# Cross value sums on eight blocks in one place, and the causal mask added inside a fused maximum

## What is computed

```python
att = jnp.einsum('bhqd,bhkd->bhqk', q, k) * scale
att = jnp.where(causal[None, None], att, -jnp.inf)
y = jnp.einsum('bhqk,bhkd->bhqd', jax.nn.softmax(att, axis=-1), v)
attc = jnp.einsum('bhqd,bhkd->bhqk', qc, kc) * scale
y = y + jnp.einsum('bhqk,bhkd->bhqd', jax.nn.softmax(attc, axis=-1), vc)
...
x = x + jnp.tanh(g_xattn[0]) * _L0_xattn_ref(_layernorm(x, axis=-1), ctx_512, ...)
```

## Time and profile before

| | us |
|---|---|
| median of 3 runs | 1542.45 (1542.35 to 1543.42) |
| the profiled execution | 1540.59 |
| its span, first to last instruction | 1538.5 |
| TensorE busy | 1426.7 (93%) |
| VectorE busy | 1145.7 (74%) |
| GpSimd busy | 901.9 (59%) |
| ScalarE busy | 896.0 (58%) |

### The profile page before, as it was taken

The page is one execution under the profiler, slowest core; times in us unless marked ns, Lnnn a source line. Parts: engine busy times, 40 slices in busy tenths (PEclk is TensorE's granted clock), DMA queues, the critical chain, the costliest instruction groups (busy, mean ns, idle before and its releaser), DMA issues.

```text
span 1538.5 us, 36199 instructions
## 1 busy us (share of the span) xinstructions
PE 1426.7 (93%) x11288; PEld 948.6 (62%) x11288; DVE 1145.7 (74%) x3026; ACT 896.0 (58%) x1907; POOL 901.9 (59%) x1643
## 2 busy tenths in 40 slices
PE   4899999999999999999999999999979989898997
PEld 3556556655566566555655665665546778787675
DVE  6777887878778887878788787878644555565686
ACT  3466676666667676666667666665723555565210
POOL 4245566664756666575756657475654555665782
PEclk8899999999999999999999999999999999999999
DMA  6745454545454554645464454545555565454794
GB/s 169 198 131 138 140 151 141 172 135 165 135 160 146 157 169 120 183 133 151 134 177 144 136 180 126 159 134 172 178 152 160 169 221 170 150 153 143 230 351 165
DMA packets 184123, 250.01 MB, mean 162 GB/s; under 512 B 32024, under 2 KB 134560, under 8 KB 183936
## 3 DMA queue, kind: packets, MB, share of 16 engines
q1 hardware_dynamic: 149680, 185.60, 42.0%
...
## 4 chain that ended last, share of the span: by engine, by line
PE 63%; DVE 18%; ACT 11%; issue 5%; DMA 2%; POOL 1%; SPq 0%; DVEq 0%; ACTq 0%; POOLq 0%
PE vector_bank L2025 8%; PE pv_self L1529 8%; DVE nmax L1288 7%; PE scalar_bank L1465 7%; PE vector_bank L1502 5%; PE vector_bank L1575 4%; PE vector_bank L1439 3%; PE vector_bank L1499 3%; ACT q L857 3%; PE scalar_bank L1452 2%; PE scalar_bank L1455 2%; PE scalar_bank L1453 2%; ACT parts L866 2%; PE scalar_bank L2012 2%; ACT parts L873 2%
## 5 line engine op out<-in xcount | busy, mean ns | idle before, releaser
L1288 DVE TENSOR_REDUCE nmax<-vector_bank 128x1 f32<-128x384 f32 (+4 forms) x832 | 511.2, 639 | 74.4 <-PE vector_bank L1502 70.0
L929 ACT ACTIVATE pt<-scalar_bank 128x512 f32<-128x512 f32 x640 | 362.7, 605 | 175.6 <-PE scalar_bank L1465 167.1
L746 POOL TENSOR_SCALAR_AFFINE_SELECT pt<-pt 128x256 f32<-128x256 f32 (+1 forms) x640 | 222.7, 362 | 206.4 <-ACT pt L929 184.4
L1465 PE MATMUL scalar_bank<-stack 99*64 99x512 bf16 (+4 forms) x1280 | 284.2, 319 | 2.3 <-ACT pt L929 1.0
L1502 PE MATMUL vector_bank<-stack 96*128 96x128 bf16 (+3 forms) x1024 | 244.0, 301 | 0.0
L1854 POOL DMA_INDIRECT rows<-pt x143 | 139.1, 973 | 117.3 <-DVE pt L1983 63.2
L1499 PE MATMUL vector_bank<-tri,ident_b 128*128 128x128 bf16 (+2 forms) x704 | 175.3, 249 | 21.5 <-DMA stack<-qk_scratch 10.5
L1529 PE MATMUL pv_self<-pt,vst 128*32 128x512 f32 (+3 forms) x2048 | 161.1, 438 | 0.1
L705 POOL DMA_INDIRECT rows<-xn,slot x128 | 132.8, 1037 | 44.2 <-issue 26.3
L1499 PEld LDWEIGHTS vector_bank<-tri,ident_b 128*128 128x128 bf16 x704 | 67.0, 97 | 145.2 <-DVE nmax L1288 59.9
L2025 PE MATMUL vector_bank<-pt 128*128 128x128 f32 x1144 | 151.2, 275 | 0.1
...
## 6 DMA issues: line engine op xcount, KB each, us to landing
...
```

What stands on the lines that cost most here:

```text
L746: pool.affine_select(out=v, in_=v, compare_op=ALU.is_ge, fill=0.0, base=0, pattern=pat, channel_multiplier=-1).then_inc(masked, 1)
L929: act.activation(dst, bank(kind, b, ("st", c, k))[:, :], ACT.Exp, scale=SCALE).then_inc(scalar_drained, 1)
L1288: dve.tensor_reduce(dst, src, axis=AX, op=ALU.max, negate=True).then_inc(vector_drained, 1)
L1465: return pe.matmul(out, stack[c][0:rows, head, key0:key0 + nk], stack[c][0:rows, head, q0:q0 + nq], start=True, stop=True, **kw)
```

## The change

Cross value sums. A half's cross products now stand in one place, at k = 14: eight products of 64 rows (one head's keys) by 32 output rows, the even heads on rows 0 to 63 into `pv_cross`, the odd ones on rows 64 to 127 into `pv_self`. `vcst` shrinks to 32 columns a pair, and the zeros go. ScalarE copies both banks at k = 15 (before: one at k = 18, at (1, 3) and at the end of c = 1). Since the bank `pv_self` is shared, the self products of (c, 0) move from k = 16 and 20 to 18 and 22. The turned cross sums move from the ends of the halves, the start of the next batch and (1, 6) to (0, 19), (0, 23), (1, 18) and (1, 21). `normalise` writes every second head of `yc`, which is one tile now.

Mask. For the 16 units a half with one head, TensorE's product with `tri` is left out, and VectorE's reduction is replaced by `tensor_tensor_reduce`: it adds `hidden_keys` (bf16, zeros and the triangle at its end) to the bank, multiplies by -1, writes the result back into the bank, and takes the minimum into `nmax`. GpSimd fills `hidden_keys` once.

```diff
@@ -85,7 +85,8 @@
 LN_SUMS = {(0, 21): 0, (0, 22): 1, (0, 23): 2, (1, 0): 3}
 LN_AGGREGATE = (1, 2)
 
-CUR_UNITS = {(1, 6): ("tU", 0, 1, "x"), (1, 11): ("tU", 0, 1, "s"),
+CUR_UNITS = {(1, 11): ("tU", 0, 1, "s"), (0, 19): ("tU", 0, 0, "x"), (0, 23): ("tU", 0, 1, "x"),
+             (1, 18): ("tU", 1, 0, "x"), (1, 21): ("tU", 1, 1, "x"),
              (0, 2): ("mT", 0, 1), (0, 16): ("mT", 1, 0), (1, 2): ("mT", 1, 1)}
 NEXT_UNITS = {(1, 8): ("v", 0), (1, 9): ("v", 1), (1, 10): ("vc",), (1, 13): ("xT", 0), (1, 15): ("xT", 1), (1, 16): ("mT", 0, 0)}
 LN_ROWS = {(1, 7): 0, (1, 9): 1, (1, 11): 2, (1, 12): 3}
...
@@ -181,19 +183,19 @@
         prev, cur, nxt = PARTS[kind]
         out = [("xT0", 0), ("xT0", 1)] if kind == "pro" else []
         if prev:
-            out += [("tU", 1, 1, "x"), ("tU", 1, 1, "s")]
+            out += [("tU", 1, 1, "s")]
         if cur:
             out += [("sm", 1, k) for k in range(SM_PRE)]
         for k in range(NST):
             out += besides(kind, 0, k)
         if cur:
-            out += [("tU", 0, 0, "x"), ("tU", 0, 0, "s")]
+            out += [("tU", 0, 0, "s")]
         if nxt:
             out += [("sm", 0, k) for k in range(SM_PRE)]
         for k in range(NST):
             out += besides(kind, 1, k)
         if cur:
-            out += [("tU", 1, 0, "x"), ("tU", 1, 0, "s")]
+            out += [("tU", 1, 0, "s")]
         return out
 
     def of_current(names):
...
@@ -212,10 +214,13 @@
     BY_SCALAR = [("yT", k) for k in range(KC)] + [("rT", t) for t in range(QT)]
     VD = Events(lambda kind: [n for n in vector_units(kind) if n not in BY_SCALAR], LB)
     TAKEN = Events(lambda kind: BY_SCALAR if PARTS[kind][0] else [], LB)
-    PV = Events(of_current([(w, c, g) for c in range(KC) for g in range(2) for w in ("x", "s")]), LB, credit=8)
+    PV = Events(of_current([(w, c, g) for c in range(KC) for w in ("x", "s") for g in range(2)]), LB, credit=8)
     MASKED = Events(of_current([(c, g, s) for c in range(KC) for g in range(2) for s in range(10)]), LB)
     YADD = Events(lambda kind: ([(1, 1)] if PARTS[kind][0] else []) + ([(0, 0), (0, 1), (1, 0)] if PARTS[kind][1] else []),
                   LB, credit=4)
+    NORM = Events(lambda kind: ([("s", 1, 1)] if PARTS[kind][0] else []) +
+                  ([("x", 0, 0), ("x", 0, 1), ("s", 0, 0), ("s", 0, 1), ("x", 1, 0), ("x", 1, 1), ("s", 1, 0)]
+                   if PARTS[kind][1] else []), LB)
     SPLIT = Events(of_next([0, 1]), LB)
     MSPLIT = Events(lambda kind: ([(0, 1), (1, 0), (1, 1)] if PARTS[kind][1] else []) +
                     ([(0, 0)] if PARTS[kind][2] else []), LB)
...
@@ -273,7 +278,8 @@
         VROW = HU * (D + 1) + 32 - D - 1
         vst_all = sb("vst", [P, QT * KC * HU * 32])
         vst = vst_all[:, 0:3 * QT * VROW].rearrange("p (s t w) -> p s t w", s=3, w=VROW)
-        vcst = sb("vcst", [P, 3, HU // 2, 64])
+        vcst_all = sb("vcst", [P, 3 * HU // 2 * 64])
+        vcst = vcst_all[:, 0:3 * HU // 2 * 32].rearrange("p (s a d) -> p s a d", s=3, d=32)
         nmax = [sb(f"nmax{c}", [P, QT, HU, 2]) for c in range(KC)]
         mres = sb("mres", [P, HEAD_GROUP, 2, QT])
         mparts = [sb(f"mparts{g}", [P, HEAD_GROUP, MROWS, 2, QT], BF16) for g in range(2)]
...
@@ -283,9 +289,9 @@
         ct = [ct_all[:, g, :, :] for g in range(2)]
         usum_all = sb("usum", [P, 4, T])
         usum = {(w, g): usum_all[:, 2 * g + i, :] for i, w in enumerate(("x", "s")) for g in range(2)}
-        recip = {w: sb(f"recip_{w}", [P, QT, HEAD_GROUP]) for w in ("x", "s")}
+        recip = {(w, g): sb(f"recip_{w}{g}", [P, QT, HEAD_GROUP]) for w in ("x", "s") for g in range(2)}
         y = sb("y", [P, QT, H, D])
-        yc = [sb(f"yc{g}", [P, QT, HEAD_GROUP, D]) for g in range(2)]
+        yc = sb("yc", [P, QT, HU, D])
         yT = sb("yT", [P, KC, T])
         xr = sb("xr", [P, QT, C])
         xn2 = [sb(f"xn2{i}", [P, QT, ROW]) for i in range(2)]
...
@@ -878,10 +885,12 @@
                     act.wait_ge(vector_filled, VU.upto(kind, b, ("tU", 0, g, w)))
                 elif g == 0:
                     act.wait_ge(vector_filled, VU.start(kind, b))
-                elif PARTS[kind][0]:
+                elif w == "s" and PARTS[kind][0]:
                     act.wait_ge(vector_filled, VU.upto(kind, b, ("tU", 1, 1, w)))
+                else:
+                    act.wait_ge(vector_filled, VU.start(kind, b))
                 act.wait_ge(pv_filled, PV.upto(kind, b, (w, c, g)))
-                act.activation(usum[w, g][:, :], (pv_cross if w == "x" else pv_self)[:, :], ACT.Copy).then_inc(pv_drained, 1)
+                act.activation(usum[w, g][:, :], (pv_cross if (w, g) == ("x", 0) else pv_self)[:, :], ACT.Copy).then_inc(pv_drained, 1)
 
             def turned_rows(kind, b, name):
 
...
@@ -955,16 +964,14 @@
                             finished_rows(kind, b, c, k)
                         if (c, k) == ROUTE_EXP and prev:
                             route_exp(b)
-                        if c == 1 and k == 3:
-                            unnormalised(kind, b, "x", 0, 1)
                         if c == 1 and k == 8:
                             unnormalised(kind, b, "s", 0, 1)
-                        if k == 18:
-                            unnormalised(kind, b, "x", c, 0)
+                        if k == 15:
+                            for i in range(2):
+                                unnormalised(kind, b, "x", c, i)
                     if cur:
                         unnormalised(kind, b, "s", c, 0)
                         if c == 1:
-                            unnormalised(kind, b, "x", 1, 1)
                             unnormalised(kind, b, "s", 1, 1)
                     elif nxt:
                         for i in (2, 3):
...
@@ -1090,10 +1097,10 @@
             def cross_values(kind, b):
                 ps = filled(kind, b, ("vc",))
                 twin = 1 + (LN.upto(kind, b, 0) - 1) % 2
-                for half_, col in ((0, 0), (1, 32)):
+                for half_ in range(2):
                     rows = slice(half_ * TC, (half_ + 1) * TC)
                     last = dve.tensor_tensor(
-                        vcst[rows, 0:twin + 1:twin, :, col:col + D],
+                        vcst[rows, 0:twin + 1:twin, :, 0:D],
                         ps[rows, 0:C].rearrange("p (s a i d) -> p s a i d", s=KC, i=2, d=D)[:, :, :, half_, :],
                         bcv[rows, :].rearrange("p (s a i d) -> p s a i d", s=KC, i=2, d=D)[:, :, :, half_, :], ALU.add)
                 last.then_inc(vector_drained, 1)
...
@@ -1285,6 +1292,12 @@
                         w = (qt + 1) * P
                         src = ps[:, 0:n * w].rearrange("p (h t) -> p h t", t=w)
                         dst = nmax[c][:, qt, h:h + n, 0]
+                    if what == "self" and n == 1:
+                        if (c, k) == FIRST_MASKED and kind == "pro":
+                            dve.wait_ge(mask_rows, 2)
+                        dve.tensor_tensor_reduce(ps[:, 0:w], ps[:, 0:w], hidden_keys[:, QT * P - w:], -1.0, BIG, ALU.add, ALU.min,
+                                                 dst).then_inc(vector_drained, 1)
+                        continue
                     dve.tensor_reduce(dst, src, axis=AX, op=ALU.max, negate=True).then_inc(vector_drained, 1)
 
             def max_transposed(kind, b, c, g):
@@ -1293,16 +1306,15 @@
 
             def normalise(kind, b, c, g, w):
 
-                n = 2 * YADD.upto(kind, b, (c, g)) - 2 * YADD.credit - (1 if w == "x" else 0)
                 h = HU * c + HEAD_GROUP * g
-                dst = yc[g][:, :, :, :] if w == "x" else y[:, :, h:h + HEAD_GROUP, :]
+                dst = yc[:, :, g::2, :] if w == "x" else y[:, :, h:h + HEAD_GROUP, :]
                 if w == "x":
 
-                    dve.wait_ge(y_added, YADD.upto(kind, b, (c, g)) - 2)
+                    dve.wait_ge(y_added, YADD.upto(kind, b, (c, 0)) - 1)
                 ps = filled(kind, b, ("tU", c, g, w))[:, :].rearrange("p (t j r) -> p t j r", t=QT, r=32)
-                dve.reciprocal(recip[w][:, :, :], ps[:, :, :, D]).then_inc(norm_step, 1)
-                dve.wait_ge(norm_step, n)
-                dve.tensor_tensor(dst, ps[:, :, :, 0:D], recip[w][:, :, :].unsqueeze(3).to_broadcast([P, QT, HEAD_GROUP, D]),
+                dve.reciprocal(recip[w, g][:, :, :], ps[:, :, :, D]).then_inc(norm_step, 1)
+                dve.wait_ge(norm_step, NORM.upto(kind, b, (w, c, g)))
+                dve.tensor_tensor(dst, ps[:, :, :, 0:D], recip[w, g][:, :, :].unsqueeze(3).to_broadcast([P, QT, HEAD_GROUP, D]),
                                   ALU.mult).then_inc(vector_drained, 1)
 
             def output_rows(kind, b, t):
...
@@ -1496,25 +1506,30 @@
                                          stack[c][0:STACK, h, KC0:KC0 + TC], start=True, stop=True)
                 else:
                     w = (qt + 1) * P
-                    pe.matmul(ps[:, 0:n * w].rearrange("p (h t) -> p h t", t=w)[:, :, qt * P:w], ident_b[:, :],
```

(41 more changed lines are left out.)

38 lines of the change are left out of this document (19 added, 19 removed).

## The result

The changed kernel takes 1650.08 us (1645.19 to 1664.12, 4 runs), against 1542.4 before: a ratio of 1.071, 95% interval 1.067 to 1.075, so 107.7 us slower. The forecast was 1582, at most 1612: the sign was right, the size was not. The profiled execution took 1648.92 us with a span of 1647.2.

A forecast was written before the change was run, and what follows sets the result against it. The prediction cut a batch into five links, ended by GpSimd's chain, VectorE or TensorE, with covers hiding TensorE's products. Changes summed to +2.69 us a batch, 37.7 over 14, +39.7 in all: 1582 us, range 1527 to 1612.

The forecast's parts named there:

- Link 1: Turning of sums (1, 0) to `mT` (1, 0), 24.78 us, ended by GpSimd's chain; forecast 0.35 us less a batch.
- the cover: Self products of kt 0 and 1, 1.71 us, occupy TensorE before `mT` (1, 0) while GpSimd's chain finishes.
- Link 2: From `mT` (1, 0) to the first projection of c = 1, 7.1 us; forecast +1.82 us a batch, mostly moved self products.
- Link 3: From there to the turning of the next rows, 24.3 us, ended by VectorE; forecast 0.35 us less a batch.
- Link 4: Turning of the next rows to the last self products, 9.5 us, TensorE always busy; forecast +1.57 us, bounds +0.8 to +2.4.
- The -0.10: Last term in the sum for Link 4: 0.10 us less a batch.
- The mask: VectorE's new masked maximum: within 0.1 us of the old operation; 0.07 us more each taken, 2.2 us a batch of VectorE.
- Rival C: New VectorE operation makes a second pass over the data, 19 us a batch: 1650 us or more; chance 0.04.
- The cross products: At k = 14, eight products on two row blocks overlap: 0.87 us a place, side by side in about 1 us.
- Rival B: Row blocks take turns, 0.87 us more a half, hidden in half 0: 13 us more, 1595 us; chance 0.11.
- Rival A: Work shed on TensorE, 3.7 us a batch, counts: with some 40% realised, 22 us faster, 1520 us; chance 0.19.
- Rival D: Gains and losses meet, waits at `mT` and k = 18 half as long: within 3 us of 1542; chance 0.06.

The follow-up runs named there:

- self_moved: Kernel before the change with one edit: self products of group 0 at k = 18 and 22 instead of 16 and 20; 1603.67 us, ratio 1.038.
- copy_early: Changed kernel with ScalarE's copy of the self sums (1, 0) ahead of the last exponential of half 1 instead of behind it; 1667.69 us, ratio 1.077.
- turn_quarter: `copy_order` with only one of four column blocks of each turned cross sum turned in middle batches; 1610.04 us, ratio 1.041.
- after_16: Changed kernel with the self products of group 0 back at k = 16 and 20; 1622.92 us, ratio 1.049.
- copy_order: `after_16` with ScalarE's copy of `pv_self` ahead of that of `pv_cross`; 1613.74 us, ratio 1.043.
- fill_more: Changed kernel plus, per batch, 26 idle products of 512 columns and 32 mask products on TensorE, whose results nobody reads; 1630.47 us, ratio 1.053.
- mT_late: Changed kernel with `mT` (1, 0) at (0, 18) instead of (0, 16), behind the first self products in half 0 alone; 1649.0 us, ratio 1.067.

## Why the prediction was right in its sign and wrong in its size

Per middle batch, at the full clock and in us; the forecast's term, and what the links show:

- **Link 1, -0.35: was +0.15.** The gap at `mT` (1, 0) is there with 2.18 us behind GpSimd's `split_max`, and the cover was read rightly. The gain of 0.35 came where only the products moved (-0.28 in `self_moved`) and not with the rest of the change, where GpSimd's chain is longer: its last instruction ends 24.86 us behind the start of the link, 24.38 before and 24.41 in `self_moved`. Most of this is the second `add_cross`, 1.25 us for 0.75 (rows below), and `split_max`, 1.59 for 1.28; one scatter is 0.26 shorter. The prediction took the chain as unchanged. It is not the instruction alone: in `copy_early` the same `add_cross` takes 0.74. Why they take longer beside other work is open.
- **Link 2, +1.82: was +2.08.** The products fall behind the `mT` (2.10 in `self_moved` for 1.63 summed, the term that was too small), and the turned sums cost what they take (0.66 for three quarters in `turn_quarter`).
- **Link 3, -0.35: was -0.54,** the right sign and nearly the size.
- **Link 4, +1.57: was +3.37, above its bound of 2.4, the step that failed.** I treated the move of the self products in half 0 alone. Their rows for half 1 stand in the earlier trace rows, at 652.86, and I took them as work that link 4 has in either order. They are a cover as well: behind them VectorE finished `xnT_low` and ScalarE its exponentials, and with the products later TensorE waits for these (0.68 and 0.35 in the timeline above). `self_moved` measures 1.30 for it in the kernel before, most of the 1.80 that were missed. The shares do not simply add up: taken back in the changed kernel, the move returns 0.23 (`after_16`), and 0.72 with the copies in the other order (`copy_order`), since the products then wait for ScalarE's copy of the shared bank, 1.49 and still 1.00 us. How much of link 4 the shared bank costs beyond the 0.49 of one copy, no run shows. In `copy_order` the cross products at k = 14 stand on the path as forecast (0.64 for three quarters, so some 0.87 for all, an estimate), and the turned sums for a third of the 0.86 that I had (0.22 of 0.66). The wait of 1.18 us ahead of the last self products was foreseen near 1.3, but under it there are no cross products any more. The -0.10 in the sum for this link is explained nowhere, and no run isolates it.
- **The clock: no term at all, +2.0.** This is the second step that failed. I wrote that work shed under GpSimd's chain "turns into TensorE standing idle" and costed that at nothing. It is not nothing, since the clock falls behind it: 75.1 less 73.0 us, 30 us over 14 batches by the links (0.1 us a batch had been there before), and 20 to 27 by `fill_more`, whose idle products also cost 0.25 us a batch.
- **Sum.** 2.69 was forecast, 5.1 at the full clock and 7.1 with the falls came: 14 x 7.1 = 99 of the 107.7 us. The 5.1 are already more than the upper bounds of all four links together (5.0). The spans of the two profiled executions differ by 108.7 us: 92.0 in 13 middle batches, 5.7 ahead of them and 11.0 behind, with one more middle batch among these. For the first and the last batch I had 2; further than that it is not split.
- **The mask** was right: 698 ns for 683 and a second instruction, its record 140 ns. The Trainium skill (VectorE: DVE Perf Modes, Two Vector instructions with no wait between them) has two instructions for such an operation; the trace agrees. The next instruction need not wait for the second one: in `mT_late` both start at 598.67. Rival C is out.
- **The cross products** were right: eight of them (16 records, from 595.93) start within 0.51 us and are done in 1.1. The Trainium skill (TensorEngine Tiling (Array Packing), Key Properties) lets different tiles run in parallel, and for the row blocks too the trace agrees: the first eight records start within 0.06 us. A cost of the change of tiling, which the prediction named, does not stand out beside the 1.03 us of the four products before. Rival B is out.
- **Rival A** is out: of what was shed, link 1 gave nothing back and link 3 only 0.54 us. **Rival D** is out.
- The period near 70.6 did not come. TensorE's busy time was to be 3 us a batch lower: the links without a fall have 63.5 us of it for 65.5, so 2.0, and with falls a batch has 65.0 us or more, because slow products are busy for longer.

The second `add_cross` of a batch, on GpSimd, first before:

```profile
599.49 0.75 POOL L753 TENSOR_TENSOR y<-y,yc 128x256 f32<-128x256 f32 x1
```

and after:

```profile
579.96 1.25 POOL L760 TENSOR_TENSOR y<-y,yc 128x256 f32<-128x256 f32 x1
```
